# POOL drains added behind every second expert-tile scatter-add of a fused attention and mixture-of-experts kernel

## The reference, cut to what matters

```python
def reference(x, ctx_2048, mask, Wq, bq, Wk, bk, Wv, bv, gate_w, w1, w2):   # x: (8, 256, 512) f32
    x = x + xattn(layernorm(x), ctx_2048, ...)     # 16 heads of 16, over 512 positions
    h = layernorm(x).reshape(2048, 512)            # 2048 tokens
    probs = softmax(h @ gate_w.T)                  # 8 experts
    topw, sel = top_k(probs, 2); topw /= topw.sum()
    combine = zeros((2048, 8)).at[arange, sel].add(topw)
    g, u = split(einsum('th,eoh->eto', h, w1), 2)  # 352 + 352 columns
    y = einsum('eti,ehi->eth', silu(g) * u, w2)
    return x + einsum('eth,te->th', y, combine)
```

## Time and profile before

| | us |
|---|---|
| median of three runs | 868.37 |
| the three runs | 868.93, 868.37, 865.26 |
| the profiled execution, its own time | 866.68 |
| its span, first to last instruction | 864.9 |
| outside the span | 1.8 |

### The profile page before, as it was taken

How to read it: one execution, slowest core, us unless ns; L and a number is a source line. 1 busy time by engine, 2 the same in 40 slices (tenths; PEclk the granted TensorE clock), 3 DMA queues, 4 the chain that set the end, 5 groups by cost and what they waited for, 6 DMA issues and landing times. The chain is left out here.

```text
span 864.9 us, 13001 instructions
## 1 busy us (share of the span) xinstructions
PE 800.5 (93%) x3757; PEld 369.7 (43%) x3758; DVE 560.9 (65%) x1071; ACT 326.0 (38%) x619; POOL 368.2 (43%) x392
## 2 busy tenths in 40 slices
PE   4888898999999999999999898899999999999993
PEld 2332333334333333433333331466565665665661
DVE  5678888888889889889888874346433333333331
ACT  0035465656656656656566666522000000000000
POOL 7535364565567657456665323343221221221221
PEclk9579999999999999999999998999999999999997
DMA  5744667766775865857655432454648546353432
GB/s 174 242 135 126 191 186 242 209 204 209 218 229 177 270 211 173 282 151 205 200 162 186 130 114 81 112 132 124 129 100 218 136 99 172 71 151 73 72 52 33
DMA packets 84524, 138.02 MB, mean 160 GB/s; under 512 B 14765, under 2 KB 40685, under 8 KB 84474
## 3 DMA queue, kind: packets, MB, share of 16 engines
q1 hardware_dynamic: 68970, 108.65, 41.9%
q0 software_dynamic: 7744, 17.86, 10.6%
q10 hardware_dynamic: 7760, 10.89, 4.5%
HBM read 77.36 MB, written 59.36 MB: 158 GB/s over the span
## 5 line engine op out<-in xcount | busy, mean ns | idle before, releaser
L876 ACT ACTIVATE pr<-sc 128x512 f32<-128x512 f32 x512 | 271.8, 601 | 174.8 <-PE sc L1579 169.5
L1023 DVE TENSOR_REDUCE mx<-tile 128x2 f32<-128x1024 f32 x256 | 304.0, 1213 | 40.3 <-PE tile L1591 35.3
L1579 PE MATMUL sc<-qk 100*128 100x512 bf16 x512 | 163.0, 389 | 8.9 <-DMA qk<-mxt 6.4
L1591 PE MATMUL tile<-qk 97*128 97x512 bf16 x496 | 148.7, 387 | 13.1 <-DVE mx L1023 10.4
L798 POOL DMA_INDIRECT out_dram<-xin,ids x36 | 56.3, 1565 | 223.2 <-DVE ids L1382 219.3
L1617 PE MATMUL pvb<-pr,vp 128*32 128x512 f32 x1024 | 128.8, 609 | 0.0
L1732 PE MATMUL pvb<-wring,qkf 128*128 (+1 forms) x216 | 98.7, 593 | 1.6 <-DVE qkf L1392 1.6
L1711 PE MATMUL tile<-wring,xh 128*128 x288 | 91.3, 460 | 0.0
L1711 PE MATMUL sc<-wring,xh 128*128 x288 | 91.2, 459 | 0.0
L1579 PEld LDWEIGHTS sc<-qk 100*128 100x128 bf16 x512 | 47.9, 100 | 100.1 <-ACT pr L876 31.1
L1591 PEld LDWEIGHTS tile<-qk 97*128 97x128 bf16 x496 | 40.8, 98 | 107.6 <-DVE mx L1023 43.0
(11 more groups left out here) (158 smaller groups left out, 818.3 us busy)
## 6 DMA issues: line engine op xcount, KB each, us to landing
qk<-stack_d SPq DMA_DIRECT2D x32, 768.0 KB
stack_d<-parts SPq DMA_DIRECT2D x32, 384.0 KB, 3.1
wring<-w_dram SPq DMA_DIRECT2D x32, 352.0 KB, 5.6
cin<-routed_d ACTq DMA_DIRECT2D x36, 257.0 KB, 3.6
stack_d<-parts SPq DMA_DIRECT2D x32, 256.0 KB, 3.1
pv_d<-ov SPq DMA_DIRECT2D x32, 256.0 KB, 3.5
xin<-x_dram SPq DMA_DIRECT2D x16, 256.0 KB, 5.4
cin<-ctxt_dram SPq DMA_DIRECT2D x8, 512.0 KB, 6.3
```

The lines of the kernel that those rows point to most:

```text
L876: nc.scalar.activation(pr[(8 * u + s) % NPR][:, j, :], sc[(32 * u + 4 * s + j) % NSC][:, :], ACT.Exp, scale=SCALE).then_inc(exped.sem, 1)
L1023: dve.tensor_reduce(cols, t[:, :, :], X, ALU.max, negate=True).then_inc(drained.sem, 1)
L1579: nc.tensor.matmul(sc[(32 * u + 4 * s + j) % NSC][:, :], ks[half(u)][0:ALL_ROWS, h, c * P:c * P + P], qs[half(u)][0:ALL_ROWS, h, :], start ...
L1591: last = nc.tensor.matmul(t[:, i, :], qs[half(w)][0:RAW_ROWS, h, c * P:c * P + P], ks[half(w)][0:RAW_ROWS, h, :], start=True, stop=True)
```

## The change

A wrapper `add_and_drain(n, k)` calls `add(n, k)` and, for k = 0, then issues `pool.drain()`. Tiles 6 and 7 and all tiles of POOL's loop go through it. So a DRAIN follows the scatter-add of tile 6 and of each even tile from 8 to 34: 1 + 14 = 15 DRAINs in this run. Nothing is removed and nothing else is moved; the waits and the DMAs stay as they are. The block's own DRAIN at the end stays too.

```diff
+            def add_and_drain(n, k):
+                add(n, k)
+                if k == 0:
+                    pool.drain()
+
...
-            add(6, 0)
-            add(7, 1)
+            add_and_drain(6, 0)
+            add_and_drain(7, 1)
             pool.wait_ge(x1_kept.sem, x1_kept.total())
             pool.wait_ge(plan_made, ALL_PLANNED)
             count = pairs(pool)
-            other_tiles(pool, add, count)
+            other_tiles(pool, add_and_drain, count)
             pool.wait_ge(y_added, count * 32)
```

## The result

In twelve runs of each kernel taken together, the changed one has a median of 858.59 us (854.6 to 861.14) and the one before 865.42 us (859.81 to 868.93). The ratio is 0.9933, with a 95% interval of 0.9911 to 0.9956: 5.8 us faster on 865.4, with 3.8 to 7.7 for the interval. (The two medians themselves lie 6.83 us apart, within that interval.) The forecast was 5.0 us, on a starting point of 862.5 + 5.0 = 867.5 us, 2.1 us above the 865.42 of the longer series. So the absolute 858.59 lies 0.9 us under the stated range of 859.5 to 867.5, while the forecast difference lies within the interval of the measured one.

A forecast was written before the change was run, and what follows sets the result against it. PE was taken to set the loop's pace, with POOL's 5.63 us DRAIN holding the core at the end. Saving 5.4 us there and losing 0.4 in the tail gave -5.0 us: 862.5 us, range 859.5 to 867.5.

The forecast's parts named there:

- The 5.63 us at the end: POOL's DRAIN at the block's end: claimed to pay for 68 indirect DMAs issued earlier, 0.083 us each.
- The DRAIN at the end, 0.2 us taken: Block's end: with one DMA behind it, 0.2 us including a floor like the start's DRAIN, so 5.4 us saved.
- The tail, +0.4 us: From tile 34's issue to the span's end: the DRAIN behind tile 34 puts tile 35's issue off by 0.4 us.
- The sign named for it: Gap from tile 34's landing to tile 35's issue should grow from 0.80 to about 1.2 us.
- The DRAIN behind tile 6, between 0 and 1 us late: Ahead of the loop: 39 DMAs cost 3.2 us, so the next scatter-add comes at most about 1 us late.
- The loop hides its DRAINs: 14 DRAINs of two DMAs, 0.17 us past the landing each, cost nothing; behind late landings scatter-adds slip some 0.4 us.
- the room of 1.1 us: Loop, behind a late landing: time left between the last copy of `finish` and PE's weight load.
- The sum: Whole kernel: -5.4 us at the end and +0.4 us ahead of tile 35 make -5.0 us.
- The starting point: Time before the change: between the profiled execution's 866.68 us and a median 1.7 us above it.
- Rival 1: The 5.63 us belong to the block's end, not the DMAs: 866.7 to 867.1 us profiled, 868 median; chance 8 in 100.
- rival 2: Each DRAIN costs a fixed amount once any DMA was issued, beside the landing: 869.5 us; chance 3 in 100.
- Rival 3: A fixed price beginning only after the landing makes POOL the bound: +17 us, 884 us; chance 7 in 100.

The follow-up runs named there:

- e1: The changed kernel run again with no edit; ratio 0.9924 (0.9893 to 0.9955) to the kernel before.
- e3: Against the changed kernel: the DRAIN stands behind the odd tiles in place of the even ones; ratio 0.9939 (0.9911 to 0.9968) to the kernel before.
- e2: Against the kernel before: one DRAIN only, behind tile 7's scatter-add and ahead of the loop; ratio 0.997 (0.9935 to 1.0006), DRAIN at the end 2.347 us.
- e7: Against the changed kernel: a DRAIN behind every tile from 6 on; ratio 0.9942 (0.9916 to 0.9968) to the kernel before.
- The ladder: Against the kernel before: five DRAINs in the attention part, ahead of routing DMAs of units 0, 1, 3, 7 and 15; DRAINs 0.050 to 1.68 us, no time given.

## Why the prediction was right

- **The 5.63 us at the end are paid for DMAs issued earlier.** Right. With DMAs since the DRAIN before on one side and lengths with nothing in flight on the other, the points are: 0 and 0.050 us, 1 and 0.126, 2 and 0.214, 4 and 0.376, 8 and 0.691, 20 and 1.676, 28 and 2.347, 34 and 2.826, 68 and 5.630, 100 and 8.243. They lie on 0.044 + 0.082 for each DMA within 0.01 us (the 1 and the 68 are the DRAINs at the end of the changed kernel and of the one before). The forecast's 0.083 came from dividing one row by 68, and the split between a count and a fixed price was a choice that the trace of before couldn't settle.
- **The DRAIN at the end, 0.2 us taken.** It was 0.126, within the 0.1 to 0.5 stated. The floor in it was misread: the 0.173 us of the DRAIN at the start of the program hold the end of the memsets. It began at 0.32, the last memset ran from 0.34 to 0.44, and it was over at 0.50. Where nothing was running and no DMA had been issued, a DRAIN took 0.050 us.
- **The tail, +0.4 us.** Measured +0.40, and +0.58 in e1, where tile 34 took 0.18 us longer to land. From landing to issue it is 1.16 us in both against 0.80, +0.36: 0.12 for the DRAIN where 0.17 was taken, and 0.24 for the steps named, lines 792, 793 and 796, where it was 0.3. The sign named for it, about 1.2 us in place of 0.80, came.
- **The DRAIN behind tile 6, between 0 and 1 us late.** No delay showed: tile 7 was issued 8.10 us after tile 6 (628.88 and 620.78), 8.08 before. The DRAIN took 6.66 us, to 627.2, 6.4 us after the scatter-add's start and 1.65 us after its landing, against 0.12 in the loop. That is the comparison by which the forecast wanted to tell a price by the DMA from a fixed one. I had left open whether its work overlaps the landing; it does with one half (4.9 + 39 x 0.041 = 6.5 us).
- **The loop hides its DRAINs.** Right: 226.36 us for 28 tiles against 226.34, and PE without a gap. Late landings came (10.8 us in the longest DRAIN) and the further delay of a scatter-add was 0.37 us for the 0.4 taken. That PE stayed without a gap was in part luck: the latest landing was 10.5 us, 1.0 us beyond the one from which the room of 1.1 us was read, and in e3 a landing of 11.0 us made PE wait for 0.5 us.
- **The sum.** -5.23 us in the tail against -5.0, and -4.87 in e1. The terms are -5.50 for the DRAIN and +0.40 ahead of tile 35; the remaining -0.13 is of the size by which landings differ.
- **The starting point.** This was the weak term. I put 862.5 us between the profiled execution and the median of three, which makes the starting point 867.5 us. The longer series had its median at 865.42, 2.1 us lower and 3 us below that of the three. The other 1.8 us of the 3.9 by which 858.59 lies under 862.5 are the medians' distance of 6.83 in place of 5.0. The size of the gain isn't touched by this; a range in absolute microseconds should have been wider at its lower end, by the spread of the three runs.
- **Rival 1** (the price belongs to the block's end) fell with the 0.126 us, and **rival 2** (fixed for each DRAIN) with the 2.347 us of e2. **Rival 3** (a fixed 5.63 us behind each landing, slower) fell with both and with e7, where twice as many DRAINs left PE untouched.
- **The rule of the Trainium skill** that a drain waits until the engine is fully idle ("PSUM — Partial Sum Buffer", section "Engine vs sequencer instructions") tells only a part here. The ladder's DRAINs all ran on an engine whose DMAs had all landed (the last of them at 596.12, 0.3 us before the fifth DRAIN) and took 0.05 to 1.68 us; the rule has no place for the DMAs already landed. It is right in that a DRAIN holds POOL until the newest scatter-add has landed.

## What to carry to other kernels

Read what lies behind the last busy instruction: here 5.6 us of an otherwise idle core stood only in the answer for the block's closing line, outside the chain. If GpSimd issues many DMAs, its DRAIN at the end of the block costs in proportion to them, and a DRAIN put where GpSimd waits anyway moves that price under other work: the one of e2 took 3.25 us off the tail. No run here has a single DRAIN late in the loop, which might do as well as fifteen. Place it where its two halves and the register steps behind it are hidden too, that is not directly ahead of the last waits of the program.

## What the runs showed of the hardware

- A DRAIN on GpSimd costs 0.044 us + 0.082 us for each DMA that GpSimd has issued since its last DRAIN, whatever the DMA's size (64 bytes or 128 rows), although all have landed. The points are ten, from 0 to 100 DMAs. Arithmetic instructions don't count: 0.050 us behind the first units' arithmetic.
- Behind a DMA in flight, such a DRAIN ends later than the landing by half of that price: 0.12, 1.2, 1.65, 1.7 and 2.8 us for 2, 28, 39, 40 and 68 DMAs. With 100 it ended 9.8 us after the last DMA's start, which is 1.6 us of descriptor generation and the full 8.2 us.
- SyncE had issued hundreds of DMAs of its own by the end of the block and its DRAIN took 0.013 us in both kernels.
